# Two batches of an attention stage sent one behind the other through the engines, with the deviation by logarithm and exponential and the first up products taken by batch

## What is computed

```python
x = x + conv_and_scan(group_norm(x))        # L0: 4 selective scans of 16 states; ends in y @ out_proj_w
t = x.reshape(2, 256, 64)
t = t + attention(layer_norm(t))            # window of 3 tokens to each side, one head of 64
t = t + experts(layer_norm(t))              # 8 experts, top 2, hidden width 682
# attention: Q = n@Wq.T+bq, K = n@Wk.T+bk, V = n@Wv.T+bv; softmax(Q.K/8 in the window) @ V
# experts:   logits = n@router_w.T; h = silu(n@w1[e].T) * (n@w3[e].T); y = h@w2[e].T; gate-weighted sum
# layer_norm: (v - mean) / sqrt(var + 1e-5) over the 64 channels of a token
```

## Time and profile before

| | us |
|---|---|
| median of 3 runs | 205.93 (205.02 to 208.98) |
| the profiled execution | 206.06 |
| its span in the trace | 204.3 |
| attention stage, from the gate product to the first up product | 118.78 to 134.41 |

### The profile page before, as it was taken

How to read it: one execution, slowest core, us unless ns; L and a number is a source line. 1 busy time by engine, 2 the same in 40 slices (tenths; PEclk the granted TensorE clock), 3 DMA queues, 4 the chain that set the end, 5 groups by cost and what they waited for, 6 DMA issues and landing times.

```text
span 204.3 us, 2686 instructions
## 1 busy us (share of the span) xinstructions
PE 192.5 (94%) x776; PEld 87.1 (43%) x778; DVE 157.3 (77%) x266; ACT 138.3 (68%) x284; POOL 96.8 (47%) x117
## 2 busy tenths in 40 slices
PE   7799999989999998999999799989999999999992
PEld 2334644444445444454354257654323333333331
DVE  6476879999999999999999954857377564663843
ACT  3629887989999999989899415546836244253431
POOL 7766565799999879998989700000000000000000
PEclk9999999999999999999999999999999999999998
DMA  4799533438989597775856000000000000000000
GB/s 150 144 241 160 195 119 95 146 108 231 196 294 213 169 266 251 213 204 172 271 198 183 4 0 0 3 0 0 0 0 3 0 3 0 0 3 0 0 0 26
DMA packets 17661, 21.79 MB, mean 107 GB/s; under 512 B 7721, under 2 KB 9198, under 8 KB 17646
## 3 DMA queue, kind: packets, MB, share of 16 engines
q1 hardware_dynamic: 17470, 21.52, 37.3%
q10 hardware_dynamic: 176, 0.10, 0.2%
HBM read 21.35 MB, written 0.26 MB: 106 GB/s over the span
## 4 chain that ended last, share of the span: by engine, by line
PE 59%; DMA 12%; POOL 11%; issue 7%; SPq 4%; DVE 4%; POOLq 1%; ACT 0%; DVEq 0%
PE ps L1175 19%; PE ps L964 12%; PE ps L1190 11%; POOL rings L410 10%; DMA cr<-c_rows 5%; DMA c_rows<-cb 5%; PE ps L971 2%; PE ps L1068 2%; DMA w_conv<-conv_w_dram 2%; SPq L315 2%; PE ps L927 1%; PE ps L887 1%; SPq L329 1%; PE ps L990 1%; POOL du L397 1%
## 5 line engine op out<-in xcount | busy, mean ns | idle before, releaser
L410 POOL TENSOR_TENSOR rings<-rings,cr 128x512 f32<-128x512 f32 x59 | 73.7, 1273 | 11.6 <-DVE rings L691 8.1
L691 DVE TENSOR_TENSOR_SCAN rings<-rings,ps 128x512 f32<-128x512 f32 x64 | 74.4, 1203 | 0.2
L858 DVE TENSOR_TENSOR rings<-ps,si 128x512 f32<-128x512 f32 (+1 forms) x44 | 30.3, 691 | 25.8 <-ACT si L583 24.8
L583 ACT ACTIVATE si<-ps 128x512 f32<-128x512 f32 (+1 forms) x44 | 26.3, 598 | 33.1 <-PE ps L1175 32.4
L501 ACT ACTIVATE rings<-delta,a_neg 128x510 f32<-128x510 f32 x64 | 44.0, 709 | 0.7 <-DVE rings L691 0.5
L1175 PE MATMUL ps<-fd,wup 64*128 64x512 f32 (+1 forms) x176 | 41.6, 607 | 0.8 <-DVE fd L793 0.5
L964 PE MATMUL ps<-rings,flip 128*128 128x512 f32 x64 | 33.8, 612 | 2.1 <-POOL rings L410 1.9
L964 PE MATMUL ps<-rings,ident 128*128 128x512 f32 x64 | 33.5, 605 | 2.1 <-POOL rings L410 2.1
L482 ACT ACTIVATE scaled<-du_tok,b_tok 128x128 f32<-128x128 f32 x108 | 34.2, 388 | 0.2
L681 DVE TENSOR_TENSOR ps<-ps,du 128x512 f32<-128x512 f32 x37 | 24.9, 681 | 2.7 <-PE ps L990 2.0
L1175 PEld LDWEIGHTS ps<-fd,wup 64*128 64x128 f32 (+1 forms) x176 | 16.0, 182 | 24.9 <-issue 14.6
(11 more groups left out here) (211 smaller groups left out, 171.3 us busy)
## 6 DMA issues: line engine op xcount, KB each, us to landing
cr<-c_rows SPq DMA_DIRECT2D x60, 256.0 KB, 4.1
wup<-w_up_dram SPq DMA_DIRECT2D x8, 341.0 KB, 6.0
wdn<-w_down_dram SPq DMA_DIRECT2D x4, 160.0 KB
wdn<-w_down_dram SPq DMA_DIRECT2D x4, 128.0 KB
w_conv<-conv_w_dram SPq DMA_DIRECT2D x1, 384.0 KB, 4.5
xc<-x_chan_dram SPq DMA_DIRECT2D x2, 128.0 KB, 4.2
w_conv<-conv_w_dram SPq DMA_DIRECT2D x1, 192.0 KB, 3.9
xg<-x_grp_dram SPq DMA_DIRECT2D x1, 128.0 KB, 2.7
```

The costliest lines, as they stand in the source:

```text
L410: nc.gpsimd.tensor_tensor(hc[:, q], hs[:, q], cr[:, row_slot(n)] if n >= ROWS_FROM else cs[:, q], ALU.mult).then_inc(weighted, 1)
L583: nc.scalar.activation(si[0:rows, S % 2, :], ps[0:rows, BANK_H + 2 * (S % 3), :], ACT.Silu).then_inc(silu_ready, 1)
L691: nc.vector.tensor_tensor_scan(hs[:, q, :], da[:, q].rearrange("p b l -> p (b l)"), driven(q), 0.0, ALU.mult, ALU.add).then_inc(scanned, 1)
L858: nc.vector.tensor_tensor(gated[0:rows, S % GATED, :], ps[0:rows, BANK_H + 2 * (S % 3) + 1, :], si[0:rows, S % 2, :], ALU.mult).then_inc(g ...
```

## The change

The stage is written again by batch: residual, statistics, deviation, scaling, turn, copy, product, scores, maximum, exponentials, turn of the probabilities, product with the values, and the second layer norm are each a function of the batch, and each engine's list of calls sets in which order the two batches take turns. ScalarE works out 1/deviation as exp(-0.5 ln(var + eps)) with one table that also holds the exponential of the softmax, and VectorE subtracts and scales in one instruction per tile. The tiles dm and sd go. Copies change hands: tnT and the first two prT by VectorE, v and the last two prT by ScalarE, qk and fd of batch 0 by ScalarE and of batch 1 by VectorE. The first three steps of the experts' first pair (AHEAD = 3) are cut into halves of 256 columns: the halves of batch 0 stand in front of the turn of batch 1. The fills are cut from 3, 8, 1 and 12 to 1, 4, none and 1.

The diff, cut to its core:

```diff
+        BANKS_OP, BANKS_T, BANKS_QK, BANKS_S, BANKS_PT = (0, 1), (2, 3), (0, 1), (5, 6), (2, 0, 3, 1)
+        BANKS_PV, BANKS_F = (4, 7), (5, 7)
+        AHEAD = 3
...
-            nc.scalar.preload_act_table_set("sqrt_and_others")
-
-            act.wait_ge(var_ready, NT)
-            nc.scalar.activation(sd[:], mv[:, :, 1], ACT.Sqrt, bias=eps[:]).then_inc(sdt_ready, 1)
-            nc.scalar.preload_act_table_set("exp_and_others")
...
+            nc.scalar.preload_act_table_set("natural_log_exp_and_others")
+
+            def inverse_deviation(turn, b):
+
+                two, done = slice(2 * b, 2 * b + 2), B * turn + b + 1
+                act.wait_ge(var_ready, 2 * done)
+                nc.scalar.activation(logv[:, two], mv[:, two, 1], ACT.Ln, bias=eps[:]).then_inc(logv_ready, 1)
+                act.wait_ge(logv_ready, done)
+                nc.scalar.activation(rs[:, two], logv[:, two], ACT.Exp, scale=-0.5).then_inc(rs_ready, 1)
...
+            exponentials(0)
+            keep_v(0)
+            keep_v(1)
+            exponentials(1)
...
+            inverse_deviation(1, 0)
+            act.wait_ge(fT_ready, 1)
+            nc.scalar.activation(fd[:, 0:L], ps[:, BANKS_F[0], 0:L], ACT.Copy).then_inc(fd_kept_a, 1)
+            inverse_deviation(1, 1)
             nc.scalar.preload_act_table_set("silu_and_others")
...
+            def normalise(turn, b):
+                dve.wait_ge(rs_ready, B * turn + b + 1)
+                dve.wait_ge(var_ready, 2 * (B * turn + b + 1))
+                for t in (2 * b, 2 * b + 1):
+                    if turn:
+                        last = nc.vector.tensor_scalar(tn2[:, t], t2[:, t].unsqueeze(1).broadcast_to([P, 2, C]), mv[:, t, 0:1],
+                                                       rs[:, t:t + 1], ALU.subtract, ALU.mult)
+                    else:
+                        last = nc.vector.tensor_scalar(tn[:, t], t1[:, t], mv[:, t, 0:1], rs[:, t:t + 1], ALU.subtract, ALU.mult)
+                last.then_inc(tn_ready, 1)
...
+            row_max(1)
+            attended(0)
+            normalise(1, 0)
+            attended(1)
+            normalise(1, 1)
...
-            keep_warm(8)
...
+            keep_warm(4)
...
+            turn_tokens(0)
+            pe.wait_ge(wqk_kept, 1)
+            times_wqk(0)
+            turn_tokens(1)
+            scores(0)
+            times_wqk(1)
+            values(0)
+            turn_probabilities(0)
+            scores(1)
+            values(1)
+            pe.wait_ge(v_ones, 1)
+            attend(0)
+            turn_probabilities(1)
+            attend(1)
+            keep_warm(1, 0)
+            turn_normed(0)
...
+            def ups_ahead(s, b):
+
+                rows, at, one = tile_rows(s), ORDER[s] * P, slice(b * L, (b + 1) * L)
+                for which in range(2):
+                    weights = wup[which * C:(which + 1) * C, 0].rearrange("p e h -> p (e h)")
+                    last = nc.tensor.matmul(ps[0:rows, BANK_H + 2 * s + which, one], weights[:, at:at + rows],
+                                            fd[which * C:(which + 1) * C, one], start=True, stop=True)
+                if b:
+                    last.then_inc(up_ready, 1)
...
+            pe.wait_ge(up_in[0], 32)
+            pe.wait_ge(fd_kept_a, 1)
+            for s in range(AHEAD):
+                ups_ahead(s, 0)
+            turn_normed(1)
             pe.wait_ge(fd_kept_d, 1)
...
-                    ups(pair, s)
+                    if pair == 0 and s < AHEAD:
+                        ups_ahead(s, 1)
+                    else:
+                        ups(pair, s)
```

More of the change, by code:

```diff
@@ L557, in _ @@
[L557 to L564, removed]
@@ new lines, in exponentials, with keep_v @@
+            def exponentials(b):
+                act.wait_ge(mx_ready, b + 1)
+                for t in (2 * b, 2 * b + 1):
+                    first = (t % 2) * (L - WIN)
+                    nc.scalar.activation(pr[:, t, first:first + WIN], ps[:, BANKS_S[b], (t % 2) * WIN:(t % 2 + 1) * WIN], ACT.Exp,
+                                         bias=nm[:, t:t + 1]).then_inc(pr_ready, 1)
+            def keep_v(b):
+                act.wait_ge(v_ready, b + 1)
+                nc.scalar.activation(v[:, 2 * b:2 * b + 2, 0:C],
+                                     ps[:, BANKS_PV[b], 0:2 * C].rearrange("p (t c) -> p t c", t=2),
+                                     ACT.Copy).then_inc(v_kept, 1)
@@ L732, in over @@
                 return ap.unsqueeze(2).broadcast_to([P, ap.shape[1], n])
[L734 to L755, removed]
@@ L757, in _, with add_residual, statistics @@
-            for b in range(B):
+            def add_residual(b):
                 two = slice(2 * b, 2 * b + 2)
                 dve.wait_ge(op_ready, b + 1)
-                chain(nc.vector.tensor_tensor(t1[:, two], xt[:, two], ps[:, b, 0:2 * C].rearrange("p (t c) -> p t c", t=2), ALU.add))
+                chain(nc.vector.tensor_tensor(t1[:, two], xt[:, two],
+                                              ps[:, BANKS_OP[b], 0:2 * C].rearrange("p (t c) -> p t c", t=2), ALU.add))
+            def statistics(src, b):
@@ L761, in _ @@
                 for t in (2 * b, 2 * b + 1):
[L762 to L769, removed]
+                    last = step(nc.vector.bn_stats(st[:, t, :], src[:, t, :]))
+                dve.wait_ge(dve_step, last)
@@ L1094, in _ @@
                 sum_state(n, n)
-            keep_warm(3)
+            keep_warm(1)
             pe.wait_ge(out_in, 16)
@@ new lines, in times_wqk, with scores @@
+            def times_wqk(b):
+                pe.wait_ge(tnT_kept, b + 2)
+                nc.tensor.matmul(ps[0:C + 1, BANKS_QK[b], 0:L], w_qk[:], tnT[:, b * L:(b + 1) * L], start=True,
+                                 stop=True).then_inc(qk_ready, 1)
+            def scores(b):
+                pe.wait_ge((qk_kept_a, qk_kept_d)[b], 1)
+                for t in (2 * b, 2 * b + 1):
+                    last = nc.tensor.matmul(ps[:, BANKS_S[b], (t % 2) * WIN:(t % 2 + 1) * WIN], qk[:, t * P:(t + 1) * P],
```

157 lines of the change are left out of this document (76 added, 81 removed).

## The result

The changed kernel took **207.68 us** (median of 4 runs, 207.37 to 208.36) against 205.89 (4 runs, 205.02 to 208.98): 0.9% more by the medians, a ratio of 1.0079 with a 95% interval of 1.0043 to 1.0116. The forecast was 204.9 with a range of 203.6 to 206.9, so the range does not hold it. The profiled execution took 207.37, its span is 205.6 and its mean clock 0.989.

The account below looks back on a forecast made before the run. The attention stage was taken as a relay between engines, bound by waiting, ahead of TensorE-bound experts. Half products gain 1.3, the relay loses 0.2, the ring 0.05: 1.05 off 206.06 gives 205.0, median 204.9, range 203.6 to 206.9 us.

Parts of the forecast that it names:

- the rival with a falling clock: Rival: with 6 of 24 fills left, TensorE's clock falls and the experts' products lose 1.4 us, 206.3; chance 0.06.
- My two thirds: Share of 130.4 to 134.6 us for which TensorE would be busy: a fill, two turns, the six products.
- the sum: Whole kernel: 1.05 us off the profiled 206.06 gives 205.0; the median lies 0.13 lower, so 204.9.
- batch 1's halves start: TensorE starts the second batch's half products at 134.6 us, against 134.41 for the whole products before.
- first whole step: Fourth step of the experts' first pair: TensorE reaches it at 136.8 us, the first glu allows 136.75.
- The scalings: Pairs of fused scalings on VectorE: 0.36 us in the first layer norm, 0.49 in the second.
- Logarithm and exponential: ScalarE's 1/deviation in both layer norms: logarithm 0.30 us, exponential 0.23, with handovers 0.59 in all.
- The relay by batch loses 0.2: Batch 1's reciprocal waits on VectorE behind batch 0's scaling, so the experts' products start 0.2 us later.
- The halves at 0.43 a half step: Experts' first pair on TensorE: 256-column half steps cost 0.43 us each; the fourth step comes 1.1 sooner.
- The rival of dear halves: Rival: half products on TensorE cost up to 0.86 us a half step, 1.3 slower, 207.4; chance 0.09.
- The rival without overlap: Rival: in VectorE's single queue each wait for ScalarE delays both batches; no gain, 206.2 us; chance 0.13.
- The silu load: ScalarE's 1.28 us table load ends at 134.3, a microsecond before the first silu; rival that it holds it: 205.2, chance 0.05.

Follow-up runs that it names:

- e3_after_again: The changed kernel again with nothing edited, for a second trace; 207.02 us, ratio 1.0024 to the kernel before.
- e2_before_few: The kernel before with only its fills cut to the changed kernel's number (1, 4, none, 1); 208.39 us, ratio 1.0087.
- e4_no_ahead: The changed kernel without half products ahead (AHEAD = 0), all products of the first pair whole; 210.94 us, ratio 1.0195.
- e5: The changed kernel with nine fills around the stage's turns, none behind the six half products; 205.82 us, ratio 0.9964.
- e8: The e5 kernel with an unused tile of dm's size in dm's old place; 206.16 us, ratio 0.9979.
- e9: The e5 kernel with seven more fills at the kernel's start; 208.53 us, ratio 1.0029.
- e12: The e5 kernel timed again with nothing edited; 205.59 us, ratio 0.9945.
- e6_before_again: The kernel before, unedited, timed against itself as a control; 206.62 us, ratio 0.9975.

## Why the prediction was wrong

**The step that failed is the clock.** The forecast asked for "a clock of 1.00 throughout", and the rival with a falling clock had 0.06. It fell to 0.50 for 3.42 us, and the stage, forecast to gain 1.05, lost 0.80. Against the fall I had set that TensorE had kept the full clock at 2.58 of 3.40 busy. That row was no answer to the question. My two thirds were taken over a stretch that holds the half products themselves, and there they were about right (2.60 of 4.20 in e3_after_again); ahead of them, where the clock fell, TensorE was busy for 1.55 of 2.92, about half. And e2_before_few with its wait of 2.78 shows that the order before needs its fills as well. The chance should have been about two in ten: 4 of 20 runs carry the sign. Its price was nearly right: 1.4 was forecast, 1.60 measured (24.40 against 22.80), of which 2.93 - 1.57 = 1.36 lies in the half products and 0.69 - 0.44 = 0.25 in the turn behind them. In part that is luck, since the 1.4 was taken from a low stretch of another length, at the kernel's start. The six fills for twenty-four, which the prediction names, were the fact to price.

**The clock does not explain all of the 1.8 us by which the medians differ.** In the profiled execution it takes the stage from 0.80 less to 0.80 more. Another 0.48 lies ahead of the stage. Of the four timed runs two have a clock of 0.989 and 0.990 and two, at 207.45 and 208.36, of 0.999 and 0.996: what these two lost is not the fall. An estimate from these numbers: with 1.60 taken off the two runs with the sign the median would still be 206.9. So a second step failed, too: the sum held the convolution and the scans at their length in one execution, and the range allowed 0.5 for the scatter at its upper end, where the gate product moves by 4 us between executions. The later timings of the same kernel gave 1.0024 (0.9957 to 1.0092), so the first ratio holds a share of scatter that four runs could not show. What makes the start and the scans vary stays open: the clock at the start is a part of it (its first rise, and its fall in e4_no_ahead), but from the first convolution product to the gate product it also varies between 108.8 (the changed kernel) and 110.3 (e3_after_again) with no change in the code, and I did not find the cause.

**The mechanism held, with two terms mis-sized.** Up to the second layer norm the changed kernel's first execution serves, less the 0.48 by which its gate product is late: the first turn, forecast for 122.1, stands at 122.29, the first row maximum (125.2) at 125.43, batch 0's reciprocal (128.65) at 128.79. Behind it e3_after_again, less 0.83:

| step | forecast | measured |
|---|---|---|
| first six half products | 132.15 | 132.41 |
| batch 1's halves start | 134.6 | 134.86 |
| first whole step | 136.8 | 137.06 |
| gain, gate to down | 1.05 | 0.80 |

- *The scalings.* 0.36 and 0.49 were forecast; the rows have 0.54 (L775) and 0.60 (L772). The first lies above its upper bound of 0.48, the second inside its bounds of 0.4 and 0.76: the nearest row for the first was L785, and to go below it because no PSUM is read was wrong. The two pairs on the path to batch 0's half products cost 0.18 and 0.11 more, about the 0.26 by which every step of the table is late.
- *Logarithm and exponential.* 0.30 and 0.23 forecast, 0.29 and 0.20 measured: right.
- *The relay by batch loses 0.2.* It loses 0.47 (e4_no_ahead), by about what the same scalings cost more (0.2 + 0.29). That VectorE's second reciprocal stands behind the wait for rs was right: forecast 131.1, measured 131.74 - 0.48 = 131.26, behind a wait of 0.60 that rs ends.
- *The halves at 0.43 a half step.* Twelve records take 1.57 and eight 1.13 at full clock, so four records more cost 0.44: right. The rival of dear halves falls. In the execution with the fall the twelve take 2.93, which could be mistaken for it; the granted clock of 0.50 tells them apart.
- *The rival without overlap* falls as well: the gain is in the stage of every trace whose clock holds there (22.80 to 22.82 in e3, e5, e8, e9 and e12).
- *The silu load.* It ends at 135.30 in e3_after_again and the first silu starts at 136.44, 0.75 behind its product; 0.73 was forecast. Hidden, with 1.1 to spare. The Trainium skill ("ScalarE: Activation LUTs", What ACT_TABLE_LOAD costs) has a drain of some 1.4 with a load, which by an estimate would have held that silu to 136.7; the trace does not show it.

## What to carry to other kernels

Fills on a tile of zeros that stand in the chain may look like an obstacle, but where they lie in a relay's waits they can hold the clock: before taking them out, price one fall of the clock on the work behind them, and look at what share of the stage TensorE is busy once they are gone. Put them into waits, not in front of an instruction whose input is ready (one in the wrong place cost 0.17). When a gain of half a percent is measured over runs that scatter by one or two, compare the stage's own length in the traces first, and then run many times: here gate to down repeats within 0.02 at the same order, fills and clock, while the median of the unchanged kernel moves by more than half a microsecond from one timing to the next.

## What the runs showed of the hardware

- The same instructions with the same waits gave a fall in one execution and none in another (the changed kernel and e3_after_again: 1.55 and 1.56 of 2.92 busy ahead). What TensorE did in the rows does not decide it alone.
- The clock's first rise varies too, after the same fills: the three at 4.23 took 0.88 in one execution and 1.46 in another, and the convolution started 1.15 later. The granted clock reads 1.00 through it in both.
- The low stretches quoted here lasted 3.42 us (the changed kernel, e4_no_ahead) and 6.82 or 6.83 (e2_before_few, e4_no_ahead, e6_before_again).
- Two fused scalings of 128x64 with two operands taken per token take 0.54, more than two bn_stats of that width (0.35) and two L785 (0.48).
